# Expert groups: turn ahead of the output of the group in front, first products four groups ahead, every second output copied by VectorE

## What is computed

```python
x = x + 0.5 * _L0_ffn_ref(_layernorm(x), ...)
x = x + _L0_attn_ref(_layernorm(x), ...)
x = x + 0.5 * _L0_ffn_ref(_layernorm(x), ...)
x = x + 0.5 * _L1_ffn_ref(_layernorm(x), ...)    # experts, first time
x = x + _L1_attn_ref(_layernorm(x), ...)         # linear attention
x = x + 0.5 * _L1_ffn_ref(_layernorm(x), ...)    # experts, second time
...
def _L1_ffn_ref(x, Wr, br, W1, b1, g1, be1, W2, b2):   # 16 experts, 2 per row
    probs = softmax(x @ Wr + br);  topk_w, topk_idx = top_k(probs, 2);  topk_w /= sum(topk_w)
    h = gelu(layernorm(x @ W1[e] + b1[e], g1[e], be1[e]), approximate=False)
    y = h @ W2[e] + b2[e]
    return sum of topk_w * y over the row's two experts
```

## Time and profile before

| | us |
|---|---|
| median of 3 runs | 627.59 (627.01 to 629.43) |
| the profiled execution | 628.28 |
| its span, first to last instruction | 626.1 |
| granted TensorE clock over the span, mean | 0.896 |

### The profile page before, as it was taken

The page is one execution under the profiler, slowest core; times in us unless marked ns, Lnnn a source line. Parts: engine busy times, 40 slices in busy tenths (PEclk is TensorE's granted clock), DMA queues, the critical chain, the costliest instruction groups (busy, mean ns, idle before and its releaser), DMA issues.

```text
span 626.1 us, 9476 instructions
## 1 busy us (share of the span) xinstructions
PE 512.6 (82%) x3033; PEld 270.7 (43%) x3033; DVE 484.3 (77%) x1373; ACT 327.0 (52%) x645; POOL 142.0 (23%) x188
## 2 busy tenths in 40 slices
PE   7687979989999999899585899877797786899800
PEld 3452322322223222244252777665555454777600
DVE  6997989898888998686987666897888758666722
ACT  2345546866676676798132688744242102678700
POOL 3000020000000000000075703654000072713645
PEclk9776969999999999999786899998797878899955
DMA  5006400028815000000225295421000015273432
GB/s 202 1 1 157 91 1 1 18 67 152 248 65 136 3 1 2 1 3 2 76 106 157 87 276 154 122 64 34 2 2 1 0 58 152 70 215 85 132 95 67
DMA packets 55981, 48.62 MB, mean 78 GB/s; under 512 B 5758, under 2 KB 48190, under 8 KB 55678
## 3 DMA queue, kind: packets, MB, share of 16 engines
q1 hardware_dynamic: 35326, 31.31, 18.4%
q0 software_dynamic: 4224, 8.59, 4.8%
q10 hardware_dynamic: 16384, 8.13, 4.5%
HBM read 24.94 MB, written 20.60 MB: 73 GB/s over the span
## 4 chain that ended last, share of the span: by engine, by line
PE 49%; DVE 25%; issue 9%; POOL 7%; ACT 4%; DMA 4%; SPq 1%; POOLq 0%; ACTq 0%; DVEq 0%
PE ps L747 7%; PE ps L716 7%; PE ps L737 7%; POOL rows_in L1105 5%; DVE arena L803 4%; PE ps L1193 4%; PE ps L1216 4%; POOL arena L1130 2%; PE ps L1555 2%; PE ps L1174 2%; PE ps L1201 2%; DVE stat L249 1%; ACT arena L1687 1%; PE ps L1499 1%; PE ps L545 1%
## 5 line engine op out<-in xcount | busy, mean ns | idle before, releaser
L803 DVE TENSOR_REDUCE arena<-ps 128x1 f32<-128x512 f32 x256 | 162.2, 682 | 25.4 <-PE ps L716 25.0
L869 ACT ACTIVATE arena<-ps 128x512 f32<-128x512 f32 x256 | 138.3, 603 | 58.5 <-PE ps L737 57.1
L716 PE MATMUL ps<-arena 96*128 96x512 bf16 x256 | 98.4, 397 | 7.9 <-DVE arena L803 6.8
L737 PE MATMUL ps<-arena 99*128 99x512 bf16 x256 | 96.4, 388 | 3.3 <-DMA arena<-arena 2.7
L1105 POOL DMA_INDIRECT rows_in<-xl,route x64 | 62.6, 978 | 149.9 <-DVE route L1061 131.6
L1130 POOL DMA_INDIRECT arena<-rows_out,route x64 | 61.3, 957 | 78.9 <-DMA rows_out<-arena 52.2
L747 PE MATMUL ps<-arena 128*32 128x512 f32 x512 | 68.2, 605 | 0.6 <-ACT arena L869 0.4
L737 PEld LDWEIGHTS ps<-arena 99*128 99x128 bf16 x256 | 24.9, 99 | 73.9 <-ACT arena L869 48.9
L716 PEld LDWEIGHTS ps<-arena 96*128 96x128 bf16 x256 | 25.1, 99 | 51.7 <-DVE arena L803 34.5
L1280 ACT ACTIVATE arena<-ps,route 128x128 f32<-128x128 f32 x124 | 46.4, 460 | 1.3 <-PE ps L1201 1.2
L1327 DVE TENSOR_REDUCE arena<-arena 128x4 f32<-128x512 f32 (+1 forms) x32 | 21.2, 663 | 30.4 <-ACT arena L1270 30.3
(11 more groups left out here) (283 smaller groups left out, 853.8 us busy)
## 6 DMA issues: line engine op xcount, KB each, us to landing
arena<-rows_in SPq DMA_DIRECT2D x28, 256.0 KB, 5.3
rows_out<-arena ACTq DMA_DIRECT2D x28, 256.0 KB, 2.5
rows_in<-zerob SPq DMA_DIRECT2D x2, 1920.0 KB, 11.2
arena<-att_parts SPq DMA_DIRECT2D x12, 256.0 KB, 8.7
arena<-in_consts SPq DMA_DIRECT2D x2, 1024.0 KB, 5.8
arena<-zerob SPq DMA_DIRECT2D x1, 2048.0 KB, 12.0
arena<-att_parts SPq DMA_DIRECT2D x14, 128.0 KB, 8.2
att_parts<-arena SPq DMA_DIRECT2D x6, 256.0 KB
```

The costliest lines, as they stand in the source:

```text
L716: pe.matmul(ps[:, bank, :], a_qs[0:96, b, h, j * P:(j + 1) * P], a_ks[0:96, b, h, keys * 512:(keys + 1) * 512], start=True, stop=True).the ...
L737: pe.matmul(ps[:, score_bank(n), :], a_ks[0:99, b, h0 + h4, i * P:(i + 1) * P], a_qs[0:99, b, h0 + h4, half * 512:(half + 1) * 512], start ...
L803: nc.vector.tensor_reduce(a_nm[:, k % 2, o % 2, k // 2:k // 2 + 1], ps[:, bank, :], AX.X, ALU.max, negate=True).then_inc(a.mpu, 1)
L869: nc.scalar.activation(a_p[:, n % 16, :], ps[:, score_bank(n), :], ACT.Exp, scale=0.25).then_inc(a.ex, 1)
```

## The change

Three things change in the loops of the pair.

1. **Order on TensorE.** The second product of group u-1 now stands behind the turn of group u. So each iteration is: turn u, second product of u-1, turn-in, first product. The turn now waits for the gelu of the group in front, since that frees its bank.
2. **Lead.** From iteration 1 on, the first product is the one of group u+4 (iteration 1 has two, of groups 4 and 5, iteration 0 has group 3), and ScalarE's squares follow. ScalarE's store of a group is issued two iterations after its gelu, not one.
3. **Copies.** The outputs of groups 1, 3, 5, 7, 9, 11, 13, 15 and also 12 and 14 are copied by VectorE (L1341 of the new kernel). The even groups 0 to 10 stay with ScalarE. Copy u of VectorE stands between the sum of group u+4 and that of u+5. The copies of groups 12 to 15 stand behind VectorE's last scaling and in front of `behind()`.

The banks of the last four groups are shared out to fit. The diff (line numbers of before and after differ by its own lines):

```diff
@@ -970,9 +970,20 @@
             xt, xtc = sem("t_rows_turned"), sem("t_rows_in")
             h, sq, sqr = sem("t_hidden"), sem("t_squared"), sem("t_squares_summed")
             z, zt, ac = sem("t_normed"), sem("t_normed_turned"), sem("t_gelu")
-            y, yc = sem("t_out"), sem("t_out_copied")
+            y, yc_a, yc_v = sem("t_out"), sem("t_out_copied_by_scalar"), sem("t_out_copied_by_vector")
             ys = [sem(f"t_out_stored{k}") for k in range(4)]
             yg = [sem(f"t_out_gathered{k}") for k in range(4)]
+
+        BY_VECTOR = [g % 2 == 1 or g >= 2 * NGR - 4 for g in range(2 * NGR)]
+        FREED = 1
+
+        def wait_out_in(eng, u):
+
+            done = (BY_VECTOR * (u // (2 * NGR)) + BY_VECTOR)[:u + 1]
+            if BY_VECTOR[u % (2 * NGR)]:
+                eng.wait_ge(t.yc_v, done.count(True))
+            else:
+                eng.wait_ge(t.yc_a, done.count(False))
 
         def tiles_in(g):
             return min(4, NTL - 4 * (g % NGR))
@@ -1149,7 +1160,7 @@
 
         def moe_scalar_store(act, m, g):
             b, u = m.b, NGR * m.i + g
-            act.wait_ge(t.yc, u + 1)
+            wait_out_in(act, u)
             k = tiles_in(g)
             act.dma_start(rows_out[b].rearrange("(j p) c -> p j c", p=P)[:, 4 * g:4 * g + k, :],
                           t_y[:, u % 4, 0:k, :]).then_inc(t.ys[u % 4], 16)
@@ -1197,6 +1208,8 @@
             def turn(u):
                 g = (u - u0) % NGR
                 pe.wait_ge(t.z, u + 1)
+                if u > u0:
+                    pe.wait_ge(t.ac, u if last - u > 3 else u - 1)
                 for j in range(tiles_in(g)):
                     ins = pe.transpose(ps[:, turn_bank(last - u), j * P:(j + 1) * P], t_z[:, u % 4, j, :], cc("ident"))
                 ins.then_inc(t.zt, 1)
@@ -1206,10 +1219,8 @@
                 k = tiles_in(g)
                 pe.wait_ge(t.ac, u + 1)
                 bank = out_bank(last - u)
-                if u == last - 1:
-                    pe.wait_ge(t.yc, u - 1)
-                elif u >= u0 + 1 and u != last - 2:
-                    pe.wait_ge(t.yc, u)
+                if u > u0 and last - u != 3:
+                    wait_out_in(pe, u - 1 if last - u > 2 else u - 2)
                 regs, at = where.pop(u)
                 pe.matmul(ps[:, bank, :], pick[:, g, :], brow[:, m.b, :, 1, :], start=True, stop=False)
                 for j in range(k):
@@ -1231,25 +1242,27 @@
                 hidden(u)
                 between(u - u0)
             routed(pair[1])
-            for u in range(u0, last - LEAD):
+            for u in range(u0, last):
                 turn(u)
-                if u + LEAD + 1 < last:
-                    turn_in(u + LEAD + 1)
-                hidden(u + LEAD)
-                out(u)
-            turn(last - 3)
-            turn(last - 2)
-            out(last - 3)
-            turn(last - 1)
-            out(last - 2)
+                if u > u0:
+                    out(u - 1)
+                for v in ahead(u - u0):
+                    if v + 1 < 2 * NGR:
+                        turn_in(u0 + v + 1)
+                    hidden(u0 + v)
             out(last - 1)
 
+        def ahead(g):
+
+            first = g + LEAD + (1 if g > FREED else 0)
+            return range(first, min(g + LEAD + (1 if g >= FREED else 0), 2 * NGR - 1) + 1)
+
         def turn_bank(left):
 
-            return TURN_IN_BANKS[0] if left == 2 else TURN_BANK
+            return TURN_IN_BANKS[0] if left in (1, 3) else TURN_BANK
 
         def out_bank(left):
-            return TURN_IN_BANKS[1] if left == 2 else OUT_BANK
+            return TURN_IN_BANKS[1] if left in (1, 3) else OUT_BANK
 
         def moe_scalar(act, pair, between):
             u0 = NGR * pair[0].i
@@ -1287,7 +1300,7 @@
                 if u >= 4:
                     act.wait_ge(t.ys[u % 4], 16 * (u // 4))
                 nc.scalar.activation(t_y[:, u % 4, 0:k, :], ps[:, out_bank(last - u), 0:P * k].rearrange("p (j f) -> p j f", f=P), ACT.Copy)\
-                    .then_inc(t.yc, 1)
+                    .then_inc(t.yc_a, 1)
 
             for u in range(u0, u0 + LEAD + 1):
                 rows(u)
@@ -1298,23 +1311,17 @@
             def store(u):
                 moe_scalar_store(act, pair[(u - u0) // NGR], (u - u0) % NGR)
 
-            for u in range(u0, last - LEAD):
+            for u in range(u0, last):
                 gelu(u)
-                if u > u0:
-                    store(u - 1)
-                if u + LEAD + 1 < last:
-                    rows(u + LEAD + 1)
-                squares(u + LEAD)
-                out_in(u)
-            gelu(last - 3)
-            store(last - 4)
-            gelu(last - 2)
-            out_in(last - 3)
-            gelu(last - 1)
-            store(last - 3)
-            out_in(last - 2)
+                if u > u0 + 1:
+                    store(u - 2)
+                if u > u0 and not BY_VECTOR[u - 1 - u0]:
+                    out_in(u - 1)
+                for v in ahead(u - u0):
+                    if v + 1 < 2 * NGR:
+                        rows(u0 + v + 1)
+                    squares(u0 + v)
             store(last - 2)
-            out_in(last - 1)
             store(last - 1)
 
         def moe_vector_tiles(dve, vs, pair, behind):
@@ -1325,6 +1332,14 @@
                 dve.wait_ge(t.sq, u + 1)
                 at, pos = place(u)
                 nc.vector.tensor_reduce(t_ss[:, at, pos:pos + k], t_sq[:, u % 2, 0:k, :], AX.X, ALU.add).then_inc(t.sqr, 1)
+
+            def out_in(u):
+                k = tiles_in(u)
+                dve.wait_ge(t.y, u + 1)
+                if u >= 4:
+                    dve.wait_ge(t.ys[u % 4], 16 * (u // 4))
+                nc.vector.tensor_copy(t_y[:, u % 4, 0:k, :], ps[:, out_bank(last + 1 - u), 0:P * k].rearrange("p (j f) -> p j f", f=P))\
+                    .then_inc(t.yc_v, 1)
 
             def place(u):
 
@@ -1352,10 +1367,14 @@
                 groups = range(max(u, u0), min(u + 1, last) + 1)
                 for v in groups:
                     summed(v)
+                    if v == groups[0] and v >= u0 + 5:
+                        out_in(v - 4)
                 dve.wait_ge(t.sqr, groups[-1] + 1)
                 vs.finish(Chain(rstds(groups[0], groups[-1])))
                 for v in groups:
                     scaled(v)
+            for v in range(last - 3, last + 1):
+                out_in(v)
             behind()
 
         def moe_vector_add(dve, vs, m):
@@ -2291,7 +2310,7 @@
                 if k == 2:
                     moe_tensor_scales(pe, m3[1])
             moe_tensor(pe, m3, between_m3)
-            pe.wait_ge(t.yc, 2 * NGR)
+            wait_out_in(pe, 2 * NGR - 1)
 
             def turned_before(g):
                 pe.wait_ge(l.y, 2)
```

## The result

| | before | changed kernel |
|---|---|---|
| median of all its runs, us | 628.51 (627.01 to 630.51) | 638.2 (635.31 to 639.24) |
| ratio, 95% interval | | 1.0137 [1.0105, 1.0168] |
| profiled execution, us | 628.28 | 637.68 |
| its span, us | 626.1 | 635.9 |
| mean granted TensorE clock | 0.896 | 0.890 |

The account below looks back on a forecast made before the run. TensorE's own work was taken to bound the middle of a pair, VectorE's chain into the adds the first pair's end. 628.28 + 4.5 + 1.0 + 0.5 = 634.3 us, 633.6 against the median; range 629.0 to 638.5.

Parts of the forecast that it names:

- The bound: Middle of a pair: TensorE's own work, 3.70 us against 3.68 between turns, which the change reorders and doesn't shorten.
- ScalarE as the pace: Rival: second products wait for ScalarE, so moving ten copies shortens a pair by up to 4.9 us; 623.2 us, chance 0.07.
- Adds of batch 0, +4.5: End of first pair: later gather and VectorE's copies delay the adds' end from 408.68 to 413.2, +4.5 us.
- the wait for copy 1: First pair: group 2's second product waits for VectorE's copy, 0.8 us kept, bounds 0 and 1.3.
- either alone would keep most of the loss: Adds of batch 0: late by 4.5 us through the gather, 3.9 through VectorE's copies alone; the larger counts.
- a term of 0.6 us: Second pair: copy 11 in front of VectorE's last chain adds 0.6 us, part of it in a wait.
- Clock in front of attention, +1.0: Linear attention's front: idle TensorE slows gate and key products, mostly hidden by VectorE's statistics; +1.0 us, bounds 0 and 4.7.
- Second pair, +0.5: Second pair: TensorE's earlier arrival at batch 1's rows only lengthens a wait; last store +0.5 us.
- GpSimd free in time: Second pair: batch 0's gather ends at 599.2, just when the last store lands (599.1), so the last gather moves by 0.5 us.
- The changed order does show: Answers the rival that the changed order doesn't show; given no chance, since nothing reorders the instructions later.
- Slack in front of attention: Rival: work behind the adds can take them 4 us later, so only the second pair counts; 628.1 us, chance 0.17.
- Late copies throughout: Rival: copy 1's 0.8 us recurs at five further copies, each pair grows by 4 us; 641.6 us, chance 0.15.

Follow-up runs that it names:

- e12: The changed kernel again with no edit, beside the kernel before: 638.28 us, ratio 1.0129.
- e5: Kernel before, with GpSimd's gather of batch 0 in the first pair also waiting for the store of group 8: 631.78 us, ratio 1.0051.
- e6: Kernel before, with VectorE waiting for all 16 output copies ahead of the adds of batch 0: 634.92 us, ratio 1.0101.
- e3: Changed kernel, with the output copies of groups 12 to 15 back on ScalarE: 636.84 us, ratio 1.0107 to the kernel before.
- e1: Changed kernel's order and lead, with all output copies on ScalarE: 633.12 us, ratio 1.0049 to the kernel before.
- e8: Changed kernel, with 12 and 6 products of zeros on TensorE before batch 0's first transposes of linear attention: 636.40 us, ratio 1.0109 to the kernel before.
- e10: Kernel before, with adds waiting for all output copies and zero products before batch 0's first attention transposes: 634.68 us, ratio 1.0062.
- e9: Changed kernel, with all copies on ScalarE, each store directly behind its copy, lead of four only from group 8: 639.06 us, ratio 1.0160 to the kernel before.
- e11: Changed kernel, with VectorE copying only groups 3, 5, 7 and 9, the rest on ScalarE: 633.87 us, ratio 1.0070 to the kernel before.
- e4: Changed kernel, with ten products of zeros ahead of TensorE's wait for group 8's rows in the second pair: 635.13 us, ratio 1.0071 to the kernel before.
- e2: Kernel before, old order and lead, with VectorE copying the outputs of groups 1, 3, 5, 7, 9 and 11: 636.13 us, ratio 1.0094.

## Why the forecast was right, and where it was off

The forecast added 4.5, 1.0 and 0.5 us, 6.0 in all; the profiled execution is 9.4 us longer. The late adds came, the clock's 1.0 did not, and the second pair lost 5.5 us instead of 0.5.

**The bound, right.** Steady turns stand 3.7 us apart after the change too, and ScalarE's waits for TensorE's second products shrank to 2.4 us over four copies (24.3 before) with no gain of time. It waits for the first products instead, in front of every one of its 32 squares; before, that wait was 13.0 us over 7 (view of waits, changed kernel):

```profile
ACT arena L1283 <- PE ps L1204: 32.8, 32, 2.5
ACT arena L1302 <- PE ps L1227: 2.4, 4, 0.8
```

ScalarE as the pace, the one faster rival, had no trace.

**Adds of batch 0, +4.5, right.** They end at 413.06 where 413.2 was forecast, 4.4 us later in the span, of which 1.04 was there when the pair began; in e12 they end 5.1 us later behind the pair's start. So the agreement to 0.1 us is luck; behind the pair's start it is 3.4 and 5.1 us in the two profiles, around the 4.5. The gather began at 390.55 (390.7 forecast), and the wait for copy 1, which no row of before had shown, was 0.93 us (0.8 forecast). e5 and e6 each put one of the two paths into the kernel before, and each alone made it slower, 0.5% and 1.0%; e3 freed one of them in the changed kernel and the adds ended no earlier. That "either alone would keep most of the loss" is shown for the gather by e3 and e1 (adds 3.4 and 2.9 us later) and for VectorE's queue by e6 (4.2). The wait of 1.09 us for copy 11 was forecast only in the second pair, inside a term of 0.6 us; it stands in both pairs of all five profiles with the new order and that copy on VectorE. In the first pair the forecast set against it the 0.7 us that the first product of group 14 comes earlier.

**Clock in front of attention, +1.0, near zero in the changed kernel.** The granted clock fell to 0.50 from 412 to 420 us, and the gate products took 3.59 us, where the forecast had 0.8 us more than 1.96. No run shows its 1.0 us: 0.8 of it is the difference between the gate products of the two batches in the earlier trace rows, and the rest was the author's estimate. The drop was deeper than taken, but the stretch to the second pair kept its length to 0.03 us (and -0.15 in e12). e8 removed the drop and won 0.7 us. Against it, e6 and e10 differ by 2.8 us in that stretch. With the adds late and the front not filled, it lies between 116.9 (e9) and 119.6 us (e6); filled, it is 116.8 both times. So the price lies between 0 and 2.8 us by the execution, within the forecast's bounds of 0 and 4.7.

**Second pair, +0.5, the step that failed.** It measured +5.5 by the landmark table (0.74 + 2.85 + 0.78 + 1.12). Its sentence was: "It would now be there one turn and one second product earlier, 1.85 us, and that is only a longer wait." The wait became longer, as said, but not for that reason alone: TensorE came to it 0.5 us earlier behind the pair's start (28.1 us against 28.6), since a new wait of 0.87 us for copy 1 stood in front, which the forecast had priced in the first pair and not here; and the rows came 0.7 us later, since their load took 3.38 us (3.44 in e12) where the earlier trace rows has 2.69. And a longer wait wasn't all. Behind the waits of 0.87 and 2.14 us TensorE's granted clock fell to 0.50 for 6 us, and that is the 2.85 us: in the five profiles of the table under e12 without such a fall after the change (e1, e11, e3, e8, e4) the stretch is 25.97 to 26.63 us, as before. That it was the two waits together that brought the fall is argued from which profiles have it; no run isolated it, since e4, meant for this, had no wait to fill. What the forecast lacked was one more question: it had weighed the clock in the front of attention, where the earlier trace rows show such a drop, and not at the one other place where it lengthened a wait itself. The term's failure is also partly that of an execution: e8 and e3, with the same code there, have no fall.

The smaller terms of the pair: the rows' load, +0.7. The tail took 0.8 more, with the wait for copy 11. And the end of the gather of batch 0 and the last store met. The forecast had computed both ends to 0.1 us (599.2 and 599.1) and called GpSimd free in time. In the changed kernel they are 607.75 and 608.45, in e1 603.10 and 603.05, and the 2.56 us of gap stayed behind either. It is a tie, not a cover. The last store also landed in 3.63 us instead of 2.59, with the gathers of batch 0 beside it. That the gathers slowed it is argued from their place only, and e10 speaks against it as the whole cause: its last store took 3.10 us, issued 4.1 us after the last of those gathers had begun.

**The rivals.** The changed order does show: from 563.52 us on the chain of waits has turn (L1214), second product (L1225, L1227), turn-in (L1185) and first product (L1202, L1204) one behind the other. Slack in front of attention: the order and lead alone (e1) cost 0.5% although TensorE's pairs were 1 to 2 us shorter. Its adds, 2.9 us late, are followed by a stretch only 0.4 us shorter than before, so there is next to none for the adds. Late copies throughout: not in the changed kernel, where only copies 1 and 11 are waited for, and that is what the lead of four buys. In the old order (e2) it is just what happens, 3.7 us in the first pair. What the runs don't give is a clean sum: by ratios order and lead are 0.5% of the 1.4, four unawaited copies 0.2 more, and copies 1, 11 and the tail's the rest with the clock drop seen behind them, each with an interval of 0.4 to 0.7%.

## What to carry to other kernels

When a reordering makes an engine arrive earlier at a wait, price the clock behind the wait, not the wait alone: here a wait that grew from 0.87 to 2.14 and 2.12 us was followed by some 6 us at a granted clock near 0.50, in the changed kernel's two profiles. Before you read a remedy's run as a proof, look in its trace whether the thing that it remedies was there. Before moving an instruction ahead, ask what else is queued behind the one that it passes, a store on which a gather waits, a copy behind which adds stand; here both held the same adds, and removing one of them (e3) brought nothing. And where two chains end within 0.1 us of each other, neither is a cover for the other.

## What the runs showed of the hardware

At group 8 of the second pair TensorE's granted clock stayed at 1.00 behind the one wait of 0.87 us (before), and fell to 0.50 behind the waits of 0.87 and 2.14 us (changed) and of 0.90 and 2.12 us (e12). It stayed at 1.00 behind 0.92 and 0.24 us (e3), and behind 0.86 and 0.83 us with no second wait (e8, e4). In e9 it fell to 0.50 from 566 to 568 us with no wait for the rows, behind waits of 1.18 us at 556 and 1.30 us at 565 for the scaling, so the fall isn't bound to that one wait. In the changed kernel the fall went on while TensorE worked without a gap: it was at 0.50 from 562 to 568 with TensorE busy 2.00 of each 2 us. The share of the span at half clock differs between executions of one kernel (in the first pair of the changed kernel it was 0.50 from 350 to 356 us in one profile and 1.00 there in e12, where it was 0.61 and 0.54 from 368 to 372), and a good part of the spread of times goes with it: of the kernel before, in e5's session, the two shortest executions (623.83 and 624.01 us) have a mean clock of 0.898 and 0.901, the two longest (634.16 and 635.63) 0.882 and 0.883. It is not so from kernel to kernel: e9 has 0.899 at 638.57 us, where TensorE lost its time in waits.
